# Order of two roots, a copy and a reciprocal on ScalarE and VectorE in a fused attention and FFN kernel

## What is computed

```python
q, k1, k2, v1, v2 = (heads(x + x @ W.T + b) for each of five projections)
S1, S2 = k1^T v1 / n, k2^T v2 / n;  S12 = S1 * S2
out = (q @ S1 * mean(v2)) * g1 + sum(S12) * g2 + (q @ S2 * mean(v1)) * g3 + (q @ S12) * g4
out = layernorm(out) * ln_g + ln_b
x1 = layernorm(x + out @ Wo.T + bo)
h = relu(x1 @ w1[0] + b1[0]);  y2 = x1 + h @ w2[0] + b2[0]
result = layernorm(x1 + layernorm(y2) * gamma + beta)
```

## Time and profile before

| | us |
|---|---|
| runs | 211.89, 212.45, 213.16 |
| median | 212.45 |
| the profiled execution, whole | 211.5 |
| its span, first to last instruction | 209.8 |
| busy in the span: PE | 194.1 (93%) |
| PEld | 178.2 (85%) |
| DVE | 163.1 (78%) |
| POOL | 136.3 (65%) |
| ACT | 127.7 (61%) |
| mean granted TensorE clock, share of full | 0.979 |

### The profile page before, as it was taken

One profiled execution on the slowest core, in us unless ns is written; L12 is line 12 of the kernel. 1 busy time (PEld: TensorE's weight loads), 2 busy tenths in 40 slices (PEclk: granted clock), 3 DMA queues, 4 the chain that ended last, 5 costly groups with the idle time before them and its releaser, 6 DMA issues.

```text
span 209.8 us, 4250 instructions
## 1 busy us (share of the span) xinstructions
PE 194.1 (93%) x1377; PEld 178.2 (85%) x1377; DVE 163.1 (78%) x478; ACT 127.7 (61%) x383; POOL 136.3 (65%) x177
## 2 busy tenths in 40 slices
PE   6969999999999999999999999999999999999930
PEld 6958998989898879887999999998989899888620
DVE  0272863989879896989698877898798869896895
ACT  0332439373758665966597577847585659786571
POOL 8904652474797749875986579755987398676130
PEclk9979999999999999999999999999999999999995
DMA  5989600000001100110010101010011001011012
GB/s 152 258 186 288 170 0 5 2 0 5 0 2 48 53 2 0 55 50 0 0 53 10 42 3 50 2 53 0 2 50 55 0 0 53 3 49 53 2 50 100
DMA packets 12116, 9.98 MB, mean 48 GB/s; under 512 B 727, under 2 KB 9950, under 8 KB 12094
## 3 DMA queue, kind: packets, MB, share of 16 engines
q1 hardware_dynamic: 11056, 8.52, 13.2%
q0 software_dynamic: 448, 0.92, 2.6%
q10 hardware_dynamic: 590, 0.26, 0.6%
HBM read 5.51 MB, written 4.19 MB: 46 GB/s over the span
## 4 chain that ended last, share of the span: by engine, by line
PE 60%; DVE 19%; issue 8%; ACT 5%; DMA 3%; ACTq 2%; POOL 1%; DVEq 0%; POOLq 0%
PE down_ps L901 19%; PE up_ps L901 16%; PE prep_ps L901 11%; PE z_ps L901 9%; DVE st L700 3%; DMA bv_rows<-in_L_attn_bv 3%; DVE y2n L705 2%; PE turn_ps L1028 2%; DVE down_ps L749 2%; PE turn_ps L999 2%; DVE z_ps L799 2%; DVE x L705 2%; ACT hT L597 1%; DVE x1T_lo L837 1%; ACT PQ_hi L573 1%
## 5 line engine op out<-in xcount | busy, mean ns | idle before, releaser
L901 PE MATMUL down_ps<-w_sb,hT 128*128 128x128 f32 x496 | 61.1, 277 | 0.1
L901 PEld LDWEIGHTS down_ps<-w_sb,hT 128*128 128x128 f32 x496 | 58.4, 192 | 1.2 <-DVE y2n L705 0.4
L597 ACT ACTIVATE hT<-up_ps,cols 128x512 f32<-128x512 f32 x64 | 41.6, 682 | 3.6 <-PE up_ps L901 3.5
L509 POOL TENSOR_TENSOR x1b<-x,b_rows 128x512 f32<-128x512 f32 x16 | 20.5, 1284 | 19.1 <-DVE x L705 19.1
L901 PE MATMUL up_ps<-x1T_hi,w_hi 128*128 128x512 f32 x64 | 26.0, 406 | 0.5 <-ACT hT L597 0.5
L580 ACT ACTIVATE res<-y,nb,rstd 128x128 f32<-128x128 f32 x60 | 24.6, 482 | 2.1 <-POOL nb L471 2.1
L901 PE MATMUL up_ps<-x1T_lo,w_hi 128*128 128x512 f32 x64 | 25.5, 398 | 0.0
L901 PE MATMUL up_ps<-x1T_hi,w_lo 128*128 128x512 f32 x64 | 25.3, 396 | 0.0
L558 ACT ACTIVATE z_sq<-z_ps 128x128 f32<-128x128 f32 x64 | 16.9, 272 | 12.3 <-PE z_ps L901 12.2
L483 POOL TENSOR_TENSOR y2g<-y2n,gamma_rows 128x512 f32<-128x512 f32 x14 | 18.0, 1286 | 8.4 <-DVE y2n L705 8.4
L498 POOL TENSOR_TENSOR xu<-X,u_rows 128x512 f32<-128x512 f32 x16 | 19.0, 1188 | 5.2 <-DVE u_rows L696 5.2
(11 more groups left out here) (151 smaller groups left out, 423.7 us busy)
## 6 DMA issues: line engine op xcount, KB each, us to landing
X<-in_L_attn_x SPq DMA_DIRECT2D x8, 512.0 KB, 9.6
out<-res SPq DMA_DIRECT2D x15, 256.0 KB, 2.0
w_sb<-in_L_ffn_w POOLq DMA_DIRECT2D x2, 256.0 KB, 9.7
out<-res SPq DMA_DIRECT2D x2, 128.0 KB, 1.9
w_raw<-in_L_attn_Wv ACTq DMA_DIRECT2D x2, 64.0 KB, 2.6
w_raw<-in_L_attn_Wk SPq DMA_DIRECT2D x2, 64.0 KB, 3.9
bv_rows<-in_L_attn_bv ACTq DMA_DIRECT2D x2, 64.0 KB, 6.3
g_row<-in_L_attn_g ACTq DMA_DIRECT2D x4, 0.1 KB
```

Source lines behind the costliest of these rows:

```text
L509: pool.tensor_tensor(x1b2[(s + 1) % 2][:, :, :], x1[:, :, :], rows(b2_rows[:, :]), ALU.add).then_inc(x1b2_out, 1)
L597: act.activation(hT[:, k, :], up_ps[k % len(up_ps)][:, :], ACT.Relu, bias=cols[:, 5 + k:6 + k]).then_inc(relu_out, 1)
L901: return pe.matmul(o, lhsT, rhs, start=start, stop=stop)
```

## The change

On ScalarE, `xT_upper(n + 2)` moves from behind std2 to directly behind the four relus, and std4 moves from there to behind std2. The order relus, std4, std2, xT_hi becomes relus, xT_hi, std2, std4. On VectorE, the reciprocal of the result (`result_factors`) moves from ahead of `xT_rest` to behind the reciprocal rstd2 and ahead of the wait for it, in front of the normalisation to x1. In step 14, which has no `xT_upper`, only the two roots and the two reciprocals change places. Step 15 stays as it is.

```diff
@@ -617,10 +617,8 @@
                     relu(st, 1)
                     relu(st, 2)
                     relu(st, 3)
-                if st.prev2:
-
-                    wait(act, st4_out, n - 1)
-                    std(two(st4, 2), std4, std4_out, 1.0 / C)
+                if st.nxt2 and st.n >= 0:
+                    xT_upper(n + 2)
                 if st.n == -1:
                     xT_upper(1)
                     gram_out(2)
@@ -630,8 +628,10 @@
                     wait(act, st2_out, n + 2)
                     wait(act, r2_out, n + 1)
                     std(two(st2, 2), std2, std2_out, 1.0 / C)
-                if st.nxt2 and st.n >= 0:
-                    xT_upper(n + 2)
+                if st.prev2:
+
+                    wait(act, st4_out, n - 1)
+                    std(two(st4, 2), std4, std4_out, 1.0 / C)
                 if st.prep:
                     PT_copy(st.prepared())
                 if st.ready is not None:
@@ -802,8 +802,6 @@
                     last.then_inc(y1_out, 1)
                     wait(dve, y1_out, m + 1)
                     stats(y1_pairs, st2, st2_out)
-                if st.prev2:
-                    result_factors(n - 2)
                 if st.nxt2 and st.n >= -1:
                     xT_rest(n + 2)
                 if st.nxt:
@@ -811,6 +809,11 @@
                     m = n + 1
                     wait(dve, std2_out, m + 1)
                     dve.reciprocal(rstd2[:, :], std2[:, :]).then_inc(r2_out, 1)
+                if st.prev2:
+                    result_factors(n - 2)
+                if st.nxt:
+
+                    m = n + 1
                     wait(dve, r2_out, m + 1)
                     wait(dve, x1T_done, m)
                     wait(dve, x1beta_out, m)
```

## The result

| | before | after |
|---|---|---|
| median of 18 runs each, us | 211.84 | 209.75 |
| ratio, 95% interval | | 0.9915 (0.9888 to 0.9943) |
| the profiled execution, whole | 211.5 | 209.8 |
| its span | 209.8 | 208.1 |
| first transposes of x1 (end of the start-up) to the end of the span | 180.65 | 179.51 |

The last row of the table holds the key to that. All changed instructions stand behind the first transposes of x1 (the row of L999 or L1002 that starts at 29.13 before and at 28.56 after). (The spans are taken from the traces to a hundredth: 209.78 and 208.07.) From there to the end the two profiles differ by 1.14 us; the other 0.57 us lie in the start-up, where no instruction was moved.

The account below looks back on a forecast made before the run. TensorE was taken to bound the kernel, waiting for x and V_sb in steps without Gram products. Savings of 0.39 + 0.39 + 0.15 = 0.93 us took 212.45 to 211.5 us (chance 0.62), range 210.4 to 213.0.

Parts of the forecast that it names:

- What bounds the kernel: TensorE holds 60% of the chain; it waits 1.5 us for x in three places, 1.5 for V_sb in four.
- xT_hi, xT_lo, rstd2, x1 in odd steps: xT_hi behind the last relu makes x1 end 0.94 us earlier; TensorE's 0.50 wait goes, 0.49 to spare.
- rstd4 for 0.05: The result's reciprocal behind rstd2 on VectorE: costs between nothing and 0.17 us, taken as 0.05.
- What is late next: V_sb in steps 4 and 6 limits next: 0.39 us saved per two-step stretch, 0.78 in two, at least 0.5.
- 0.39 of the 0.50: Step 6's product with E_sb starts 0.39 us earlier; the rest of the 0.50 becomes longer waiting for V_sb.
- Steps 13 and 14: Step 13's 0.51 us wait goes, step 14 cuts the gain: 0.15 taken, between 0.23 saved and 0.2 lost.
- at most 0.23 comes through: Step 14: x1T_hi waits 0.23 us for TensorE behind result activations, so no more of step 13's gain survives.
- Sum: Whole kernel: 0.39 + 0.39 + 0.15 = 0.93 us saved.
- Base and range: Median of the runs shown, 212.45, less 0.93 gives 211.5 us; range 210.4 to 213.0, medians up to half a us off.
- (a): Rival: TensorE's waits outside the start-up and step 2 go for good, 1.85 us saved, 210.6; chance 0.14.
- (b): Rival: nothing moves, something else holds x1 or queues differ; within 0.3 us of 212.4; chance 0.18.
- (c): Rival: slower, later result holds x1T_hi in steps 3, 5, 13, 14; up to 214.3 us; chance 0.06.

Follow-up runs that it names:

- e9: Kernel before with xT_hi directly behind the relus in step 0 alone: 180.51 us from the first transposes to the end, against 180.65; one run only, 211.30.
- e4: Changed kernel with VectorE making E_sb and V_sb behind two of four y2n tiles in even steps: 178.06 us behind the start-up, ratio to before 0.9886.
- e5: Changed kernel with the old order of roots and reciprocals in step 14 only: 179.28 us from the first transposes to the end, against 179.51.
- e1: Changed kernel again, unaltered, beside the kernel before: median of 12 runs 210.51 us, ratio 0.9943; 179.49 us behind the start-up.
- e3: Kernel before with VectorE's part alone (result's reciprocal last, ScalarE's order as before): 180.91 us behind the start-up against 180.65, ratio 1.0052.

## Why the prediction came out as it did

*What bounds the kernel:* right, with a gap. The three waits for x and the waits for V_sb were read rightly, but I took TensorE's list of waits for complete. Step 0 was not costed by itself, though VectorE has no idle time behind xT_lo there, and 0.15 us in step 1 came of it (e9). My own working had the gap in hand: it put 0.13 us of the stretch of steps 1 and 2 into TensorE's first half of step 1 and asked no further.

*xT_hi, xT_lo, rstd2, x1 in odd steps:* right. I had xT_lo at the statistics' end, rstd2 0.60 later, the normalisation 0.21 after that, and 0.49 to spare; the trace has 0.59 and 0.21, and x1 ends at 90.87, 0.50 before the down product's end at 91.37.

*rstd4 for 0.05:* it cost nothing in odd steps, and 0.1 in step 14, where std4 wasn't there in time. I took from the Trainium skill ("VectorE: DVE Perf Modes", "The DRAIN you can't avoid") that a next op waits for an empty pipe, and that is not what this trace shows for the pair: rstd4 starts 0.09 after rstd2, which takes 0.17. I had left out how that section of the Trainium skill goes on: a next op that is not held starts earlier, and it points to "Two Vector instructions with no wait between them" for which ones are held. With that the trace agrees.

*What is late next:* right, and the best part of it. I forecast 0.39 per stretch of two steps and a wait for V_sb near 0.5. Measured: 22.13 - 21.74 = 0.39, 22.14 - 21.74 = 0.40, and 0.51. From the sum's start to the product with E_sb it took 95.76 - 91.40 = 4.36, where I had 4.35. Only "0.39 of the 0.50" was no good picture: 0.66 was gained at the transposes and 0.26 given back. e4 shows that V_sb alone took the rest.

*Steps 13 and 14:* 0.15 forecast, 0.22 measured (1.14 in all less the 0.92 that was there by step 13). The mechanism that I named, rstd4 late and the result ahead of x1T_hi, is there but is the smaller part; the later x1 in step 14 I hadn't seen. My bound, "at most 0.23 comes through", was wrong: with the old order in step 14 about 0.41 does (e5), since the result does not stay where it was, as the bound supposes: it starts 1.50 us earlier there, the transposes 1.36.

*Sum:* 0.93 forecast. In the part behind the start-up it is 1.14 to 1.20 between profiles, and about 1.2 in runs of equal clock. The term missing is step 0's, 0.15; the rest is the 0.07 of steps 13 and 14.

*Base and range:* this is the step that failed. I put the sum onto 212.45, the median of three runs, and allowed half a us for how far such a median can be off. What the runs show in its place is a start-up that comes in two kinds: the groups by mean clock lie 1.7 us apart (210.29 and 212.00 for the kernel before), and a median goes where the shares of the two take it. The profile had half clock in the start-up, and the three runs all lie in the upper half of the 18 that were made in the end, whose median is 211.84; later sets of 29, 23 and 23 runs of the same kernel had 211.12, 211.48 and 210.38. On 211.84 my sum gives 210.9, inside the range. Of the 1.16 that then still separate 210.9 from 209.75, some 0.2 are the terms that I had too small; the rest is of the size that the start-up makes, and 10 of the 18 runs of the changed kernel had a mean granted clock of 0.985 or more. No profile shows the start-up of each run, so that division is argued from the mean clocks. The changed kernel's other set (e1) had 4 such runs of 12 and a median of 210.51, inside my range: on which side of 210.4 the median fell was luck. That those shares are the change's doing is not shown: 34 of 75 runs before and 16 of 30 after lie below 0.985. The window that shows the half clock stood in the profile of before (granted clock 0.57 from 13 to 17 us), and I had read windows only from 39 us on.

*The rivals:* (a), that the waits go for good, was wrong by V_sb's 0.51. (b) was wrong. (c) did not happen in the changed kernel, where x1T_hi is ready (92.44) 0.37 before x1T_lo starts (92.81), but it did in e3, where the same delay has no earlier x1 to hide it.

## What to carry to other kernels

When a copy waits in a queue behind small operations whose inputs are later than its own, put it first, and move with it whatever stands between it and its reader on the other engine: one half alone gave half the gain, the other half alone a loss. Ask where the chain behind the removed wait ends next, and cost the gain by a step in which that wait is already absent. A gain under 1% needs a reading that leaves out the start-up's spread: compare profiles from one fixed instruction to the end, or runs of equal granted clock. And before you put a range around the median of a few runs, look in the profile for stretches that can go one way or the other.

## What the runs showed of the hardware

TensorE stands idle for 0.4 to 2.3 us at a time between 10 and 14 us, for the small transfer into late_rows, for V_sb and for ScalarE's Wog; behind that it is granted half clock (1.2 GHz) for 3.4 or 6.8 us in some executions and not at all in others, and the first transposes of x1 then come anywhere between 27.9 us (e3) and 31.5 (e1). With eight spare matmuls in those gaps they came at 27.8 to 28.2 in all four profiles, and 3 of 36 runs had a mean clock under 0.985, where it is 34 of 75 for the kernel before as it stands.

"TensorE: Matmul & The Clock Gate" in the Trainium skill, section "What's actually happening", says that idle time brings the array to half its clock and activity releases it. These runs agree in so far as filling the idle gaps made the half clock rare. They don't show how much idle time it takes: the profile of before had gaps of 0.69, 0.67 and 0.43 us and then half clock, while the profile of after had 2.21 and 0.63 and kept the full clock.

The rest of the kernel is steady by comparison: equal steps of different executions agree within 0.03 us.
